# An order table for a mixer and feed-forward kernel on Trainium2: due times shifted by two tables, and the account's DMA rate and delays set anew

## What is computed

```python
# mixer (N=16 states, D=2048 channels, H=1024)
u, gate = split(x @ W_in.T)
u  = silu(causal_conv4(u) + conv_b)
dt, B, C = rmsnorms(split(u @ Wx.T, [64, 16, 16]))
delta = softplus(dt @ Wdt.T + dt_bias)
state_t = exp(delta_t * A) * state_{t-1} + (delta_t * u_t) * B_t   # D x N states
y_t = sum_n state_t[:, n] * C_t[n]
x = layernorm(x + ((y + u * D_param) * silu(gate)) @ W_out.T)
# feed-forward with routed low-rank adapters
scores = x @ gate_w.T + gate_b            # four ranks: 8, 16, 32, 64; the best one is taken
x = layernorm(x + x @ W.T + b + (x @ A[:r].T @ B[:, :r].T) for the chosen r)
```

## Time and profile before

| | |
|---|---|
| time, median of 3 runs | 2220.3 us |
| profiled execution, its own time | 2226.45 us |
| its span | 2224.7 us |
| TensorE busy | 92% |
| VectorE busy | 89% |
| GpSimd busy | 81% |
| ScalarE busy | 66% |
| mean granted TensorE clock | 0.967 |
| adds on VectorE / on ScalarE and GpSimd | 714 / 246 |

### The profile page before, as it was taken

How to read it: one execution, slowest core, us unless ns; L and a number is a source line. 1 busy time by engine, 2 the same in 40 slices (tenths; PEclk the granted TensorE clock), 3 DMA queues, 4 the chain that set the end, 5 groups by cost and what they waited for, 6 DMA issues and landing times. The chain is left out here.

```text
span 2224.7 us, 30702 instructions
## 1 busy us (share of the span) xinstructions
PE 2054.6 (92%) x10528; PEld 1555.2 (70%) x10528; DVE 1972.6 (89%) x2385; ACT 1475.2 (66%) x2179; POOL 1802.1 (81%) x767
## 2 busy tenths in 40 slices
PE   8989999999979798999989988999999998797998
PEld 6867778787656577777865547787875556584586
DVE  3448899999989999999999999999899998899953
ACT  4478787777566776776876566676786566756531
POOL 4369998888998999878899987987689997698850
PEclk9989999999989899999999999999999999998999
DMA  8867856553323357654543323574464337344340
GB/s 290 284 232 252 302 173 202 172 178 119 98 90 98 113 177 263 220 184 152 186 159 102 109 90 116 171 270 158 142 199 120 111 97 235 100 142 137 105 143 39
DMA packets 168764, 363.23 MB, mean 163 GB/s; under 512 B 18656, under 2 KB 45408, under 8 KB 168608
## 3 DMA queue, kind: packets, MB, share of 16 engines
q1 hardware_dynamic: 168608, 361.26, 49.7%
HBM read 292.35 MB, written 68.85 MB: 162 GB/s over the span
## 5 line engine op out<-in xcount | busy, mean ns | idle before, releaser
L1566 POOL TENSOR_TENSOR drive<-delta_u,b_bcast 128x2048 f32<-128x2048 f32 (+1 forms) x257 | 1172.2, 4563 | 111.6 <-PE state_t L935 106.2
L1118 DVE TENSOR_TENSOR_SCAN drive<-decay,drive 128x512 f32<-128x512 f32 x1024 | 1192.3, 1205 | 48.4 <-ACT decay L1358 28.1
L1358 ACT ACTIVATE decay<-delta,a_sb 128x512 f32<-128x512 f32 x1024 | 694.2, 688 | 383.2 <-DVE drive L1118 379.2
L935 PEld LDWEIGHTS state_t<-identity,drive 128*128 128x128 f32 x4096 | 486.8, 144 | 271.2 <-DVE drive L1118 108.0
L935 PE MATMUL state_t<-identity,drive 128*128 128x128 f32 x4096 | 582.3, 281 | 80.8 <-DVE drive L1118 63.7
L967 PE MATMUL bank<-cols_high,w_split 128*128 128x512 f32 (+1 forms) x1240 | 525.1, 423 | 28.8 <-DMA w_split<-w_split 6.7
L1126 DVE SCALAR_TENSOR_TENSOR y_acc<-state_t,c_rows,y_acc 128x512 f32<-128x512 f32 x714 | 506.7, 735 | 46.2 <-PE state_t L935 43.5
L969 PE MATMUL bank<-cols_high,w_split 128*128 128x512 f32 (+1 forms) x1240 | 492.3, 397 | 0.0
L968 PE MATMUL bank<-cols_low,w_split 128*128 128x512 f32 (+1 forms) x1240 | 490.0, 395 | 0.0
L990 PE MATMUL bank<-channels,w_raw 128*128 128x512 f32 x896 | 423.7, 600 | 3.4 <-POOL channels L1587 3.4
L1571 POOL TENSOR_TENSOR y_acc<-y_acc,scaled 128x512 f32<-128x512 f32 x246 | 316.2, 1285 | 116.3 <-ACT scaled L1378 112.7
(11 more groups left out here) (204 smaller groups left out, 1452.4 us busy)
## 6 DMA issues: line engine op xcount, KB each, us to landing
w_split<-w_split SPq DMA_DIRECT2D x304, 512.0 KB, 3.9
b_bcast<-b_rows SPq DMA_DIRECT2D x256, 256.0 KB, 3.5
w_raw<-in_w_out SPq DMA_DIRECT2D x112, 256.0 KB, 3.0
w_raw<-in_w_in SPq DMA_DIRECT2D x64, 256.0 KB, 4.6
gates<-scratch SPq DMA_DIRECT2D x64, 256.0 KB, 3.8
scratch<-gates SPq DMA_DIRECT2D x64, 256.0 KB, 4.9
rows<-in_x_rows SPq DMA_DIRECT2D x4, 2048.0 KB, 9.6
out<-rows SPq DMA_DIRECT2D x16, 512.0 KB, 3.3
```

The lines of the kernel that those rows point to most:

```text
L935: last = engine.transpose(bank[0:tile.shape[1], i * P:(i + 1) * P], tile, identity[:, :])
L1118: engine.tensor_tensor_scan(state, decay[(GT * s + t) % DECAYS][:, :], state, 0.0, ALU.mult, ALU.add).then_inc(signal["scan"])
L1358: engine.activation(decay[i % DECAYS][:, :], delta[:, g % 2, t, :], ACT.Exp, scale=a_sb[:, j, n:n + 1]).then_inc(signal["decay"])
L1566: engine.tensor_tensor(drive[key % DRIVES][:, tiles, :], du[:, tiles, :], row, ALU.mult).then_inc(signal[stage])
```

## The change

Every piece's due time is shifted by half the sum of two numbers: one by its stage and its sequence (`STAGE_SHIFTS`; for `x_load` by its tile), one by the job it belongs to (`JOB_SHIFTS`: a group, a channel tile, a weight). The tables have 427 and 757 numbers. The account's `RATE` goes from 300 to 270, `DELAY` from 0.25/0.13/0.13/0.15/2.0 to 0.3/0.14/0.14/0.14/2.2 for PE/DVE/ACT/POOL/SP, and `decay` is accounted with 0.63 instead of 0.605. `or_mm` gets a need on the same product of the time tile before; the weight is given back with the product of the last time tile. No instruction's work changes; their order, the buffers used and the way each add is done may.

```diff
--- before.py
+++ after.py
@@ -102,6 +102,210 @@
             self.reached[id(semaphore)] = value
+STAGE_SHIFTS = {
+    "x_load": (-37, 45, -58, 133, 92, 35, -37, -27),
...
+    "raw_load": (-9, 49, 13, -15),
...
+    "consts": (78,),
...
+    "u_mm": (-92, 2, 0, -16),
...
+    "or_vnorm": (-37, -54, 153, -78),
...
+    "xr_low": (22, 22, -145, 9),
...
+    "drive": (-1, 10, 1, -44),
+    "decay": (0, 11, 20, -11),
+    "scan": (76, 0, -3, 50),
+    "turn": (14, -45, -125, -1),
...
+    "add": (35, -1, -31, 36),
+    "scale": (48, -24, -26, -79),
+    "sum": (-24, -3, 65, -113),
+}
+JOB_SHIFTS = {
...
+    "split": (
+        (-76, -13, 3, 37), (-25, -56, -44, -5), (-160, -5, -19, 26), (-9, 9, 8, 22), (-25, -3, 2, 18), (-57, 0, 5, 16),
...
+    "drive": (21, 1, -134, 109, 101, -9, -34, 131, 16, -56, 45, 130, 134, 85, 61, -47),
...
+    "scan": (58, -3, 46, 70, 4, 52, -10, 113, -1, 38, 51, 74, 81, -7, 71, 133),
+    "turn": (-66, 38, 71, 64, 22, 1, 21, -72, -76, 8, -52, -8, -129, -146, -9, -40),
...
+    "add": (99, 10, 67, -24, -5, 2, 3, -75, -12, 4, -37, -50, -101, -6, -33, 103),
+    "scale": (62, -155, -81, -133, -17, -56, -107, -71, -103, -11, -29, 16, -16, -52, 16, -22),
+    "sum": (-16, -135, -68, -101, 10, -7, -137, -49, -163, -157, -47, -8, -148, -95, -61, -49),
+}
+def job_of(stage, key):
+    if stage in ("drive", "drive_begun", "fetch", "decay", "scan", "turn", "first", "add", "scale", "sum"):
+        b, g, _ = UNITS[key if stage in ("drive", "drive_begun", "fetch") else key[0]]
+        return b, stage, b * NG + g
+    b = key[0] if isinstance(key, tuple) else key
+    if stage in ("softplus", "delta_mm", "du"):
+        return b, "delta", b * NG + key[1]
+    if stage in ("y_turn", "y_skip", "y_gate", "g_load"):
+        return b, "y", b * NG + key[1]
+    if stage in ("u_mm", "u_tap", "u_conv"):
+        return b, "u", b * DT + key[1]
+    if stage == "u_silu":
+        return b, "silu", b * DT + key[1]
+    if stage in ("g_mm", "g_copy"):
+        return b, "g", b * DT + key[1]
+    if stage in ("g_silu", "g_store"):
+        return b, "gates", (b * DT + key[1]) // 2
+    if stage == "raw_load":
+        kind, (what, n) = key
+        if kind == "x":
+            return what, "x", what * HT + n
+        if kind == "w":
+            return n - 1, "split", (what[0], n - 1)
+        return n - 1, what[0], (what[1] if len(what) > 2 else 0, n - 1)
+    if stage in ("w_load", "w_high", "w_low", "w_store", "dt_rest"):
+        return key[1] - 1, "split", (key[0][0], key[1] - 1)
+    if stage in ("x_high", "x_low", "x_first"):
+        return b, "x", b * HT + key[1]
+    if stage.startswith("o_"):
+        part = key[2] if stage != "o_mm" else [key[2] in tiles for tiles in OUT_PARTS[b]].index(True)
+        return b, "out", (b * HT + key[1]) * 2 + part
+    if stage.startswith("f_"):
+        return b, "ffn", b * HT + key[1]
+    if stage.startswith("x1_"):
+        return b, "x1", b * HT + key[1]
+    return b, None, 0
+def shift_of(stage, key):
+    b, job, i = job_of(stage, key)
+    shift = STAGE_SHIFTS[stage][b]
+    if job:
+        row = JOB_SHIFTS[job]
+        shift += row[i[0]][i[1]] if isinstance(i, tuple) else row[i]
+    return 0.5 * shift
 class Plan:
@@ -114,9 +318,9 @@
               "ln1_sqrt": "sqrt", "ln2_sqrt": "sqrt", "or_table": "sqrt", "or_sqrt": "sqrt", "fr_table": "sqrt", "fr_sqrt": "sqrt"}
     CHANGE = 1.28
-    RATE = 300.0
-
-    DELAY = {"PE": 0.25, "DVE": 0.13, "ACT": 0.13, "POOL": 0.15, "SP": 2.0}
+    RATE = 270.0
+    DELAY = {"PE": 0.3, "DVE": 0.14, "ACT": 0.14, "POOL": 0.14, "SP": 2.2}
     def __init__(self):
         self.pieces, self.work = {}, {e: [] for e in ENGINES}
@@ -130,7 +334,7 @@
         assert (stage, key) not in self.pieces, (stage, key)
-        self.pieces[stage, key] = dict(engine=engine, due=due, us=us, name=(stage, key), needs=list(needs), take=list(take),
+        self.pieces[stage, key] = dict(engine=engine, due=due + shift_of(stage, key), us=us, name=(stage, key), needs=list(needs), take=list(take),
                                        give=list(give), spare=spare, kb=kb, order=len(self.pieces), ahead_of=ahead_of)
     def either(self, add, scale):
@@ -425,7 +629,8 @@
             if tt == 0:
                 weight[half, k] = split_weight((TILES + half, k), due, ("or_mm", (TT - 1, half, k)))
             w, there = weight[half, k]
-            put("PE", due, 0.69, "or_mm", key, [there, y_low_of(k)] + ([("or_mm", (tt, half, k - 1))] if k > OUT_ROWS[0] else []),
+            put("PE", due, 0.69, "or_mm", key, [there, y_low_of(k)] + ([("or_mm", (tt, half, k - 1))] if k > OUT_ROWS[0] else []) +
+                ([("or_mm", (tt - 1, half, k))] if tt else []),
                 take=[("bank", ("or_mm", (tt, half)))] if k == OUT_ROWS[0] else [], give=[("split", w)] if tt == TT - 1 else [],
                 spare=1 if k == OUT_ROWS[0] else 0)
         put("ACT", at, 0.22, "or_table", LAST, [("decay", (len(UNITS) - 1, GT - 1))])
@@ -570,7 +775,7 @@
             [("turn", (s - DRIVES, tt)) for tt in range(TT)] if s >= DRIVES else [("lora_rest", 0)] + [("x_first", (0, k)) for k in range(HT)]))
         for t in range(GT):
             i = GT * s + t
-            put("ACT", i - DECAYS - 0.5, 0.605, "decay", (s, t), [("softplus", (b, g, t // 2))] + (
+            put("ACT", i - DECAYS - 0.5, 0.63, "decay", (s, t), [("softplus", (b, g, t // 2))] + (
                 [("scan", divmod(i - DECAYS, GT))] if i >= DECAYS else []))
             put("DVE", i, 1.13, "scan", (s, t), [drive_of(s, t), ("decay", (s, t))],
```

More of the change, by code:

```diff
@@ L102, in wait_ge @@
             self.reached[id(semaphore)] = value
+STAGE_SHIFTS = {
+    "x_load": (-37, 45, -58, 133, 92, 35, -37, -27),
+    "x_high": (-55, -10, 29, 45),
+    "x_first": (63,),
+    "raw_load": (-9, 49, 13, -15),
+    "w_high": (-9,),
+    "dt_rest": (-136,),
+    "w_store": (61,),
+    "consts": (78,),
+    "lora_high": (4,),
+    "lora_rest": (-19,),
+    "rows_load": (-111, -139, 113, 147),
+    "w_low": (-20,),
+    "u_mm": (-92, 2, 0, -16),
+    "u_tap": (-34, -159, -105, 33),
+    "u_conv": (51, -49, 1, -73),
+    "u_silu": (152, -101, -91, -74),
+    "ssm_mm": (122, 5, -48, -111),
+    "ssm_square": (-13, 123, -70, -87),
+    "ssm_stat": (-92, -150, -94, -131),
+    "ssm_sqrt": (-66, -150, -83, 31),
+    "ssm_dt": (-41, -190, 7, -58),
+    "ssm_norm": (144, -112, -105, 43),
+    "ssm_turn_dt": (110, -135, -143, 82),
+    "ssm_turn_b": (-56, -108, -120, 178),
+    "dt_cols": (-8, 34, -103, 153),
+    "dt_low": (76, -14, -6, -112),
+    "b_cols": (101, 142, 41, 129),
+    "b_store": (-133, -140, -32, -55),
+    "delta_mm": (0, 1, 1, -56),
+    "softplus": (9, 87, 25, 27),
+    "g_mm": (4, 2, 13, 3),
+    "g_copy": (-8, -26, 22, 3),
+    "g_silu": (-89, 153, 14, -71),
+    "g_store": (43, 27, 132, -30),
+    "x_low": (0, -46, -47, -88),
+    "w_load": (0, 0, 18, -20, -114),
+    "o_mm": (-7, -7, -10, 38),
+    "o_copy": (-48, 44, -67, 33),
+    "o_turn": (-4, -56, -127, 55),
+    "o_add": (-67, -15, -153, -37),
+    "ln1_stats": (-91, -11, 103),
+    "ln1_sqrt": (125, -19, 19),
+    "ln1_rstd": (26, 61, -130),
+    "ln1_bias": (62, 143, 110),
+    "ln1_norm": (-61, -55, -65),
+    "x1_turn": (58, 50, 125),
+    "x1_high": (81, -30, -39),
+    "x1_low": (-43, -90, 28),
+    "route_mm": (11, -138, -100, -158),
+    "route_lift": (158, -14, -33, -1),
+    "route_rows": (-123, -101, -35, 105),
+    "route_max": (-46, 28, 104, -1),
+    "route_exp": (138, -16, 120, 6),
+    "route_pick": (-99, -32, -141, -70),
+    "route_mask": (-7, -105, -60, -27),
+    "route_turn": (2, -5, 119, 20),
+    "lora_cols": (45, -100, 15, -22),
+    "lora_low": (-52, -151, -14, 8),
+    "f_mm": (1, -32, 89),
+    "f_lora": (13, -105, -68),
+    "f_copy": (-105, 64, -15),
+    "f_turn": (11, -97, -91),
+    "f_add": (36, -30, -33),
+    "ln2_stats": (2, -65, -72),
+    "ln2_sqrt": (-57, 145, 1),
+    "ln2_rstd": (-59, -75, -97),
+    "ln2_bias": (-95, 117, -111),
+    "ln2_norm": (66, -129, -134),
+    "y_high": (0, 0, 0, 0, 0, 0, 0, 0, -100, -110, 104, 146, 63, -24, -69, 158),
+    "y_rest": (0, 0, 0, 0, 0, 0, 0, 0, 2, -75, 59, 192),
+    "y_low": (0, 0, 0, 0, 0, 0, 0, 0, 0, 0, 0, 0, 106, 38, -99, -126),
+    "or_mm": (0, 3, -9, 1),
+    "or_table": (0, 0, 0, -104),
+    "or_add": (55, -113, 58, -90),
+    "or_stats": (-118, 54, 8, -40),
+    "or_sqrt": (-5, -68, -6, -180),
+    "or_rstd": (-59, -176, -48, -155),
+    "or_norm": (147, 29, 133, -77),
+    "or_vnorm": (-37, -54, 153, -78),
+    "xr_turn": (-76, 115, 63, 127),
+    "xr_high": (-114, -104, 109, 153),
+    "xr_low": (22, 22, -145, 9),
+    "fr_table": (0, 0, 0, -136),
+    "wf_load": (-31, 118),
+    "bias_load": (20,),
+    "fr_bias": (-145, 1, -38, -64),
+    "fr_mm": (-156, -118, 154, 135),
+    "fr_lora": (-96, -32, 111, -57),
+    "fr_add": (91, -27, 92, -87),
+    "fr_stats": (148, -10, 238, 79),
+    "fr_sqrt": (-154, -18, 120, 96),
+    "fr_rstd": (115, 46, 55, -162),
```

(19 more changed lines are left out.)

22 lines of the change are left out of this document (added), and 7 rows, old and new, of the table JOB_SHIFTS.

## The result

The changed kernel takes 2152.4 us (median of 4 runs, 2150.82 to 2156.92) against 2221.38 us of the kernel before beside it; the ratio is 0.9689 (95% interval 0.9675 to 0.9702). That is 69 us less. The forecast was 32 us less (2188 us), its range 2145 to 2232: the direction and the range held, the size did not. The profiled execution has a span of 2149.3 us, 75.4 less than that of before.

What follows compares the result with a forecast made beforehand. The prediction took VectorE to bound the 1977 us stage of the units, with TensorE close behind. Its terms, -11 - 20 + 2 - 3 + 0 = -32 us, took 2220.3 us to 2188 us, with an 8-in-10 range of 2145 to 2232.

Steps and rivals of the forecast that it cites:

- Idle time of VectorE in the stage: Stage of the 256 units: VectorE waits less for turns (43.5 us) and decays (28.1 us), -20 us.
- the bound of -72: Stage of the units: the far bound of the idle-time term, all 71.6 us of waits for turns and decays gone.
- turns 31 earlier and a more faithful account: Stage of the units: ready turns pass background products on TensorE; new constants let queues hold work in between; together -20 us.
- Adds moved: Stage of the units: 16 adds go from VectorE to ScalarE and GpSimd, 0.69 us each, -11 us.
- Lead: Before the first scan: new order of x tiles leaves 2 x 2 k steps behind TensorE's gap, +2 us.
- Tail: After the units: last row's square root and normalization (L1234) come earlier, so the feed-forward's first product does too, -3 us.
- Need of `or_mm`: Added need on the same product of the time tile before: nothing waits behind it, 0 us, bounds 0 and +1.
- much faster: Rival, chance 0.14: order also fills TensorE and raises its clock, half of VectorE's idle time goes, 2140 us.
- Slower: Rival, chance 0.18: turns wait longer for scans in TensorE's in-order queue and hold up everything behind, 2245 us.
- point of decision: The slower rival decides from an idle time of VectorE in the stage above 116 us.
- Nothing is left: Rival, chance 0.12: mean shifts cancel, adds stay near 246 and VectorE's idle time near 104 us, 2218 us.
- The prediction's signs for the stage: VectorE busy under 1873 - 7 us, share above 95%, line 1571 above 255 times, turn waits below 35 us, GpSimd busier.

Runs made afterwards that it cites:

- b2: Changed kernel with its constants, but only mean shifts of scale, sum, add, drive, scan and turn, the same for all units, everything else 0: 2243.0 us.
- a1: Changed kernel with every shift set to 0, leaving the account's new constants and the added need of `or_mm`: 2241.1 us, ratio 1.0079 to the kernel before.
- a3: Changed kernel with its constants and, of the shifts, only those of add, scale and sum, all others 0: 2253.0 us.
- d1: Kernel before, order untouched, without the product of the rows with the low half of the columns on TensorE: 2208.6 us, stage 1969.5 us (before 1972.9).
- b4: Changed kernel with its constants and all shifts except those of the unit chain (fetch to sum): 2304.1 us, ratio 1.0369 to the kernel before.
- d2: Kernel before, order untouched, each `sum` on GpSimd adding only 64 of its 512 columns: 2216.5 us, stage 1963.2 us (before 1972.9).

## Why the prediction was wrong

- *Idle time of VectorE in the stage, -20 us:* this is the step that failed, by its size: -62 us. The prediction took a bit over a quarter of the 71.6 us of waits for turns and decays, because it held the mean wait for a turn, 0.75 us, to be the time of a turn itself and so beyond an order in most cases. About a turn's time it is (an add waits for four transposes, not 16; in the trace of before they take 0.6 us from the first one's start to the last one's end). That an order can't avoid it was the error: 42.6 went to 17.6 us and the decays' 28.1 to 5.0, so 48 us of these 71 went, two thirds. Another 14 us went from waits that the term put at nothing: for drives 4.9, the rest before the convolution, `y_skip` and the sums of the rows. The total stayed inside the bound of -72.
- *Its cause, turns 31 earlier and a more faithful account:* not borne out. Mean shifts with the constants (b2) leave the waits for turns at 42 us, the constants alone (a1) at 42, and both are slower than before.
- *Adds moved, 16, -11 us:* 10 moved and VectorE's work fell by 11 us. That the size fits is luck: ten adds at the term's 0.69 us are 7 us, and the adds' line fell by 7.9. As a gain of its own the term is not borne out either, for a3 moves 33 more than a1 and is slower by 12 us, though one order can't refute it.
- *Lead, +2 us:* +3.1 in the first scan's start, by another way. The term counted the k steps that fall behind the gap, four of them; it read ten steps ahead of the gap before where the trace has eight (24 matmuls), and missed the first matmul at 11.44 us. These and the pitch cancel, for at 80 us TensorE is one matmul behind before. What is late is the end of the lead.
- *Tail, -3 us:* -5.5, by another way: 23 more matmuls of `or_mm` are done before the last scan ends. The term's own path was read wrong: 2167.56 us is not the first product of the feed-forward, which starts at 2160.62, so a faster L1234 could give TensorE the 1.5 us of its wait and not 4. That part came true: all eight L1439 take 0.50 to 0.55 us, and the wait is gone.
- *Need of `or_mm`, 0:* right. The kernel before with this need added gets the same list for every engine, worked out without the chip.
- *Sum:* the spans give 3.1 - 62 - 11 - 5.5 = -75.4, the medians -69.
- *The rival "much faster"* (2140, chance 0.14) had the better size, half of the idle time gone, but tied it to TensorE's clock. The clock of the stage did rise from 0.97 to 0.99, and TensorE's busy time in it fell by 21 us. But d1 takes 167 us of TensorE's busy time away and has before's stage to 3 us, so 21 us less can't be the cause. *Slower* was what most neighbouring orders do (a1 to a3, b2 to b4); its point of decision, idle time above 116 us, was met by a3 and b4. *Nothing is left* had the mean shifts cancel: alone they do (b2), and that said nothing of the whole. The prediction's signs for the stage nearly all came (work below 1866 us, line 1571 above 255 times, waits for turns below 35 us): they told the direction, not the size.

What stays open: by which places of the order each wait went, what the constants are worth once tables are made for the old ones, why the chip's span lies 3 us above the account's end in one order and 35 in another, and which of the 40 us of idle time that the four fastest orders keep could still go.

## What to carry to other kernels

An order that a list scheduler (here `arrange`) writes from due times can jump with its inputs, most of all one whose tables were fitted to its account: one delay changed by 0.01 us was worth 44 us on the chip, and no part of the tables that was tried meant anything alone. Judge such a change by the end of its whole schedule and by the idle time left on the bounding engine, not by the direction or mean of its shifts; and change a constant of the account only together with new tables. Where the bounding engine idles in many waits of under a microsecond, look for ready work of that engine to stand between producer and consumer: this is what the changed lists look like, though no run tried it alone. Taking load off its neighbours under the old order (d1, d2) did almost nothing for it, and moving some of its own work away (a3) made it wait more.

## What the runs showed that I had not expected

With 190 us less of busy time on TensorE, or over 200 us less on GpSimd (1715.57 to 1486.58 in the stage), the stage of the kernel before got 3 and 10 us shorter. TensorE at 93% of a stage and GpSimd at 87% can both be far from bounding it by their load.
